# One edge of a fused decoder kernel's first batch: which buffer tile 1's V rows are gathered into, and the order of DVE and TensorE work around it

## The reference

```python
scores = jnp.einsum('bsr,nr->bsn', Q, K) / math.sqrt(K.shape[1])   # 8192 keys per token
topk_scores, topk_idx = jax.lax.top_k(scores, 8)
weights = jax.nn.softmax(topk_scores, axis=-1)
output = jnp.einsum('bskd,bsk->bsd', V[topk_idx], weights)         # 8 rows of V per token
x = _layernorm(x + output)                                         # sublayer 1
q = x @ Wq; k, v = split(context @ Wkv)                            # sublayer 2, 16 heads of 64
attn = softmax(clip(where(mask, q k^T * 64 ** -0.5, max_neg), -5, 5))
x = _layernorm(x + (attn v) @ Wo + bo)
x = _layernorm(x + expert_ffn(x))                                  # sublayer 3
```

## Time and profile before

| | |
|---|---|
| median of 3 runs | 1360.39 us (1360.38 to 1360.89) |
| the profiled execution's own time | 1361.8 us |
| its span, first to last instruction | 1360.0 us |
| PE / DVE / ACT / POOL busy | 1315.0 / 1102.1 / 729.8 / 724.7 us |
| mean granted PE clock over the span | 0.991 of full speed |
| chain that ended last | PE 88%, DVE 8%, the rest 1% or less each |

### The profile page before, as it was taken

One profiled execution on the slowest core, in us unless ns is written; L12 is line 12 of the kernel. 1 busy time (PEld: TensorE's weight loads), 2 busy tenths in 40 slices (PEclk: granted clock), 3 DMA queues, 4 the chain that ended last, 5 costly groups with the idle time before them and its releaser, 6 DMA issues.

```text
span 1360.0 us, 25400 instructions
## 1 busy us (share of the span) xinstructions
PE 1315.0 (97%) x9927; PEld 997.2 (73%) x9927; DVE 1102.1 (81%) x1628; ACT 729.8 (54%) x1377; POOL 724.7 (53%) x1009
## 2 busy tenths in 40 slices
PE   8878999999999999999999999999999999999897
PEld 4556777777878787878787878786868686867775
DVE  2389888888888888888888888888888998546567
ACT  1364555555555555555555555555555554336565
POOL 0553565656565656465656464746574746332425
PEclk8999999999999999999999999999999999999999
DMA  9561121212121212121212121212121316002412
GB/s 369 196 199 58 47 75 55 74 56 75 55 75 55 75 54 75 55 75 55 75 54 75 55 75 55 75 55 75 52 77 36 80 38 183 10 17 95 158 37 90
DMA packets 57554, 110.38 MB, mean 81 GB/s; under 512 B 9443, under 2 KB 38107, under 8 KB 56283
## 3 DMA queue, kind: packets, MB, share of 16 engines
q1 hardware_dynamic: 40326, 62.13, 14.9%
q0 software_dynamic: 14848, 41.96, 10.4%
q10 hardware_dynamic: 2260, 4.66, 0.9%
HBM read 98.50 MB, written 10.22 MB: 80 GB/s over the span
## 4 chain that ended last, share of the span: by engine, by line
PE 88%; DVE 8%; issue 1%; POOL 1%; DMA 1%; ACT 1%; SPq 0%; POOLq 0%; DVEq 0%; ACTq 0%
PE side_bank L390 51%; PE score_bank L390 33%; DVE cand_val L1304 2%; DVE cand_idx L1307 2%; PE score_bank L826 2%; DVE x_sum L1330 1%; DVE dispatchedT L1475 1%; PE side_bank L826 1%; POOL v_rows L1537 1%; DVE x L1368 1%; PE side_bank L553 1%; DMA xT_by_step<-in_xTs 0%; PE score_bank L611 0%; POOL exp L1565 0%; DMA shared_compress<-xT_by_step 0%
## 5 line engine op out<-in xcount | busy, mean ns | idle before, releaser
L976 ACT COPY score_row<-score_bank 128x512 f32<-128x512 f32 x512 | 299.2, 588 | 109.6 <-PE score_bank L390 58.9
L1304 DVE MAX8 cand_val<-score_row 128x8 f32<-128x2048 f32 x128 | 291.8, 2280 | 70.6 <-ACT score_row L976 70.6
L1537 POOL DMA_INDIRECT v_rows<-in_V,top_idx x256 | 248.4, 970 | 122.7 <-issue 70.9
L1565 POOL TENSOR_SCALAR exp<-exp,exp_bound 128x256 f32<-128x256 f32 x512 | 245.1, 495 | 97.3 <-ACT exp L988 95.5
L1307 DVE FIND_INDEX8 cand_idx<-cand_val,score_row 128x8 uint32<-128x2048 f32 x128 | 292.5, 2285 | 0.0
L390 PE MATMUL score_bank<-keysT_hi,qT_hi 128*128 128x512 f32 x512 | 215.5, 421 | 13.0 <-ACT score_row L976 11.9
L390 PE MATMUL score_bank<-keysT_hi,qT_lo 128*128 128x512 f32 x512 | 204.0, 398 | 0.0
L390 PE MATMUL score_bank<-keysT_lo,qT_hi 128*128 128x512 f32 x512 | 203.9, 398 | 0.0
L988 ACT ACTIVATE exp<-side_bank 128x512 f32<-128x512 f32 x256 | 139.0, 595 | 88.3 <-PE side_bank L390 88.3
L390 PE MATMUL side_bank<-qT_heads,kT 64*128 64x256 f32 x1024 | 145.2, 402 | 1.3 <-ACT exp L988 1.3
L1330 DVE SCALAR_TENSOR_TENSOR x_sum<-v_rows,top_weight,x_sum 128x256 f32<-128x256 f32 x256 | 130.0, 508 | 9.2
(11 more groups left out here) (200 smaller groups left out, 2303.5 us busy)
## 6 DMA issues: line engine op xcount, KB each, us to landing
kT<-den_scratch SPq DMA_DIRECT2D x62, 256.0 KB, 4.0
f_quads<-in_f POOLq DMA_DIRECT2D x32, 256.0 KB, 3.4
comp_then_wqkv_raw<-in_comp SPq DMA_DIRECT2D x6, 1024.0 KB, 19.2
xT_by_step<-in_xTs SPq DMA_DIRECT2D x4, 1024.0 KB, 8.8
xT_in<-in_xT SPq DMA_DIRECT2D x16, 256.0 KB, 3.0
keysT_raw<-in_KmT ACTq DMA_DIRECT2D x8, 512.0 KB, 20.6
x_sum<-in_x SPq DMA_DIRECT2D x32, 128.0 KB, 2.0
ctxT_in<-in_ctxT SPq DMA_DIRECT2D x16, 256.0 KB, 4.7
```

Source lines behind the costliest of these rows:

```text
L976: nc.scalar.copy(srow[n // PER % 2][:, i * CB:(i + 1) * CB], scb[n % 3]).then_inc(sem("score_evac"), 1)
L1304: own(nc.vector.max(cv[:, tile, cs], srow[g % 2][:, :]))
L1537: pool.indirect_dma_start(out=vg[:, k, :], out_offset=None, in_=V_rows, in_offset=bass.IndirectOffsetOnAxis(ap=i8[:, tile, k:k + 1], axis=0))\
L1565: last = nc.gpsimd.tensor_scalar(ex[i % NEX][:, k, :], ex[i % NEX][:, k, :], ub[:, k, c:c + 1], E_LO, ALU.min, ALU.max)
```

## The change

Four edits, all of them in turn -1:

1. `gather(0, 1)` writes into `qT_heads` and signals a semaphore of its own (`vg_ramp_in`). It no longer waits for tile 0's sum. `value_sum(0, 1)` reads `qT_heads` in place of `v_rows`.
2. On DVE, `value_sum(0, 0)` goes from behind row 6 to behind row 7 and `merge(0, 1)`. `value_norm(0, 0)` and `x1_lo(0, 0)` go into `first_sum`, the block that holds tile 1's sum, and this block stands between the MAX8 and the FIND_INDEX8 of row 9 in place of row 10.
3. On POOL, `rstd1(0, 0)` goes from ahead of tile 1's gather to behind it.
4. On PE and ACT, row 11's scores go from behind tile 0's transposes to behind the first two query projections. The fills grow from 12 to 20 and from 4 to 8.

```diff
@@ PE, ramp
                 x1_transpose(0, 0)
-                for e in range(4):
-                    score(0, e)
                 project(("K", 0, 2), 1, 4 * P, cth, ctl)
                 project(("K", 0, 3), 1, 6 * P, cth, ctl)
-                fill(12)
+                fill(20)
                 x1_transpose(0, 1)
-                fill(4)
+                fill(8)
                 need(pe, "x1_lo", TT)
                 for j in range(2):
                     project(("Q", 0, j), 0, 2 * j * P, x1h, x1l)
-                for e in range(4, 8):
+                for e in range(8):
                     score(0, e)
@@ ACT, ramp: the same four blocks move behind queries_out(0, 1)
@@ DVE, value_sum
-                    need(dve, "vg_in", 16 * TOPK * (TT * batch + tile + 1))
+                    if in_ramp(batch, tile):
+                        need(dve, "vg_ramp_in", 16 * TOPK)
+                    else:
+                        need(dve, "vg_in", 16 * TOPK * max(TT * batch + tile, 1))
+                rows = qt if in_ramp(batch, tile) else vg
                 for k in ks:
-                    own(nc.vector.scalar_tensor_tensor(acc[:, tile, :], vg[:, k, :], w8[:, tile, k:k + 1],
+                    own(nc.vector.scalar_tensor_tensor(acc[:, tile, :], rows[:, k, :], w8[:, tile, k:k + 1],
@@ DVE, first_sum and the turn
+                value_norm(0, 0)
                 value_sum(0, 1, range(TOPK))
+                x1_lo(0, 0)
                 value_norm(0, 1)
                 x1_lo(0, 1)
...
-                if mid and c:
+                if mid and c > 0:
                     value_sum(m, 0, range(TOPK))
                 candidates(c, 4)
...
                     merge(m, 1)
-                    value_norm(m, 0)
+                    if c == -1:
+                        value_sum(m, 0, range(TOPK))
+                    else:
+                        value_norm(m, 0)
                 candidates(c, 5)
...
-                candidates(c, 6)
-                if c == -1:
-                    x1_lo(m, 0)
-                candidates(c, 7, first_sum if c == -1 else None)
+                candidates(c, 6, first_sum if c == -1 else None)
+                candidates(c, 7)
@@ POOL, gather and the turn
                 if ks[0] == 0:
-                    need(pool, "sum_done", TT * batch + tile)
+                    if in_ramp(batch, tile):
+                        need(pool, "sc_stored", 16 * 4)
+                    else:
+                        need(pool, "sum_done", TT * batch + tile)
                     need(pool, "idx_done", TT * batch + tile + 1)
...
-                    if mid and h == 9 and c != 0:
+                    if mid and h == 9 and c > 0:
                         rstd1(m, 0)
...
+                if c == -1:
+                    rstd1(m, 0)
```

More of the change, by code:

```diff
@@ L250, in need, with in_ramp @@
                 eng.wait_ge(sem(name), v)
+        def in_ramp(batch, tile):
+            return batch == 0 and tile == 1
         def job_bank(key):
@@ L1049, in ramp @@
                 x1_hi(0, 0)
-                for e in range(4):
-                    score_out(0, e)
                 keys_out(0, 2)
@@ L1533, in gather @@
                 if ks[0] == 0:
-                    need(pool, "sum_done", TT * batch + tile)
+                    if in_ramp(batch, tile):
+                        need(pool, "sc_stored", 16 * 4)
+                    else:
+                        need(pool, "sum_done", TT * batch + tile)
                     need(pool, "idx_done", TT * batch + tile + 1)
+                rows, landed = (qt, "vg_ramp_in") if in_ramp(batch, tile) else (vg, "vg_in")
                 for k in ks:
-                    pool.indirect_dma_start(out=vg[:, k, :], out_offset=None, in_=V_rows,
+                    pool.indirect_dma_start(out=rows[:, k, :], out_offset=None, in_=V_rows,
                                             in_offset=bass.IndirectOffsetOnAxis(ap=i8[:, tile, k:k + 1], axis=0))\
-                        .then_inc(sem("vg_in"), 16)
+                        .then_inc(sem(landed), 16)
             def rstd1(batch, tile):
```

## The result

| | before | after |
|---|---|---|
| median of 5 runs each, same chip | 1360.39 us (1360.32 to 1363.87) | 1368.4 us (1366.41 to 1369.64) |
| ratio, with its 95% interval | | 1.004 (1.0025 to 1.0054) |
| span of the profiled execution | 1360.0 us | 1366.6 us |
| PE busy, matmuls | 1315.0 us, 9927 | 1319.1 us, 9951 |

A forecast was written before the change was run, and what follows sets the result against it. PE was taken to bound the kernel from about 141 to 1160 us. Row 11's search, 2.3 us late, would make PE 2.0 late through POOL's clips: 1360.39 + 2.0 = 1362.4 us, range 1359.8 to 1364.3.

The forecast's parts named there:

- DVE's part: In the ramp: tile 1's gather starts at 116.86, its value_norm at 134.73, x1_done comes 4.92 us earlier.
- rival C: In the ramp: tile 1's rows land late or are waited for over 2.5 us; later than 4.2 us, chance 0.04.
- where it is lost: PE's fills hold tile 1's transposes back 2.2 us; row 11's search is 2.3 late, PE 2.0 late through POOL's clips.
- so I take half clock to 131.23: PE's key projections in the ramp: 10 of 24 matmuls at 0.213 us, 14 at 0.120, ending at 132.9.
- rival A: PE in the ramp: half clock stays one more stretch; 3.5 us late in place of 2.0, 1363.9 us; chance 0.22.
- the hole: PE's wait for x1(0, 0) in the ramp, 0.9 us of the half-clock stretch; given as reason for the clock staying low.
- From then on PE, ACT and POOL run in the old pattern, 2.0 us later: After turn 0's products with v: the 2.0 us lateness is carried on, with nothing added in later turns.
- the first paragraph: Takes turn 0's products with v, at 161.71 and 168.71, as PE's last work waiting for something on DVE's schedule.
- The base: The whole kernel's time before the change, 1360.39 us, to which the forecast added 2.0 us.

The follow-up runs named there:

- e3: The changed kernel with 8 and 4 fills in place of 20 and 8; ratio to the kernel before 1.0009, median 1363.44 us.
- e4: The changed kernel, in turn 0 POOL clips heads 2 and 3 ahead of the sixth gather transfer, context's low half behind head 7; ratio 1.0030, 1366.73 us.
- e6_t14: The changed kernel with turn 14's gather split 5, 1 and 2 as in the other turns; ratio to the kernel before 1.0029, median 1366.15 us.
- e2: The changed kernel, unchanged, run once more; ratio to the kernel before 1.0040, median 1367.46 us.
- e7: The changed kernel with 8 and 4 fills, turn 0's changed order of clips and context's low half, and turn 14's gather split; ratio .9992, 1361.11 us.
- e13: The changed kernel with tile 1's transfers counted on the values' own semaphore again, new buffer kept; ratio 1.0024, 1371.74 us on another chip.
- e14: e7 with the values' own semaphore again for tile 1's transfers, new buffer kept; ratio to the kernel before .9976, 1365.78 us on another chip.
- e8: e7 with three of row 11's four blocks ahead of the key projections, 0 and 4 fills; ratio to the kernel before .9993, 1361.57 us.
- e11: The same program as e7, run again; ratio to the kernel before .9980, median 1360.26 us.
- e5: The kernel before with tile 1's gather into the query heads' buffer on its own semaphore, all orders as before; ratio 1.0010, 1363.44 us.
- e9: The kernel before with tile 1's transfers on a semaphore of their own, old buffer kept; one run, 1365.18 us.

## Why the prediction was wrong

**Right: DVE's part.** Less the 1.47 of the start, tile 1's gather began at 116.84 (116.86 forecast) and its layer norm at 134.74 (134.73). The gather was no slower in the other buffer (the layer norm behind it was on time); rival C is out.

**Right: where it is lost.** PE's fills held tile 1's transposes back, DVE idled in front of `x1_lo` (3.96 us), row 11's search was late, and the delay reached PE through POOL's clips. e3 and e4 show both links. PE's waits at turn 0's first products, 0.55 and 1.80 us, are those of the forecast (0.6 and 2.0).

**The step that failed first: "so I take half clock to 131.23".** The low clock lasted to 134.6, rival A's case, which I gave 0.22; 131.23 and the 1.47 of the start make 132.7, so PE had some 1.9 us more at half speed than I allowed. Less the 1.47: fills from 133.83 (forecast 132.9, rival A 134.16), transposes 138.30 (137.35; 138.8), row 11's search 146.79 (145.9; 147.4), batch 1's gather 154.33 (153.45; 155.0), PE in turn 0 2.96 late by the ramp's stage (2.0; 3.5). Everything from there to PE is shifted by the same 0.9 to 1.0.

That the shift stayed under A's 1.5 is luck. In after the low clock began 21.6 us behind row 6: it fell in part on row 10's last block, ahead of a wait, where it costs nothing, and the last five of the 24 key projection matmuls ran at full clock. In e6_t14, the same ramp, it began 23.0 behind and held for all 24. PE's rows there, from tile 0's transposes on:

```profile
128.93 0.69 PE L557 MATMUL side_bank<-identity,x 128*128 128x128 f32 x2 [1.01 <-DVE x L1345]
...
134.54 4.71 PE L394 MATMUL side_bank<-identity 128*128 128x128 f32 x40
139.08 0.38 PE L557 MATMUL side_bank<-identity,x 128*128 128x128 f32 x2
```

Row 6 started at 104.91 there, 0.18 later than before. Less that: fills from 134.36, transposes 138.90, batch 1's gather 154.94 (from 155.12), and the ramp's stage is 3.60 longer than before. A had 134.16, 138.8, 155.0 and 3.5.

Why the clock stayed low is open. A's reason was the hole, PE's wait for tile 0's `x`. In after, e2, e3, e4, e6, e7, e13 and e14 the low clock lasted 6.8 us, in e8 and e11 3.4, and the idle time of PE in the first half does not sort them. These are the first 3.41 us of the low clock in e7, where it stayed, and in e11, the same program, where it went (columns as in the earlier trace rows):

```profile
125.91:129.32 3.41, 3.00 (x10) 2.19 (x11) 3.23 (x6) 1.97 (x5) 0.72 (x2) 0.50 0.23 68
```

```profile
128.00:131.41 3.41, 2.79 (x13) 2.79 (x14) 3.16 (x9) 0.61 (x2) 0.00 (x0) 0.50 0.37 113
```

PE was busy for 3.00 us where the clock stayed low, and for 2.79 where it came back. The Trainium skill (TensorE: Matmul & The Clock Gate, Part 1), that being throttled is the default, had pointed towards A; eight of the ten traces of this ramp agree, and none shows what decides. (The prediction calls on two stretches of the earlier trace rows for it, but only the first of them shows what went ahead of a low clock; for the other the trace has PE busy 1.48 of the 3.42 us ahead.)

**The term that was missing: 1.7 us in turn 14.** "From then on PE, ACT and POOL run in the old pattern, 2.0 us later" is the sentence that failed. It rests on the first paragraph, which took turn 0's products as the last PE work that waits for something on DVE's schedule; the trace before has 2.2 us of such waits in turn 14. I took a second semaphore for a matter of bookkeeping. The late starts were in the trace before (3.82 where 2.40 is usual) and I read past them, because in turn 13 one costs nothing. e5 and e9 show the term alone, 1.3 to 1.4 us. e13 puts the late start back into turn 13; that the time falls with it is likely (2.2 us by the ratios, whose intervals overlap).

**The base.** 1360.39 was the median of three runs that lay within 0.5 us; more runs had a median of 1362.4 to 1363.9 on three chips. By its stages the changed kernel is 4.6 us above whatever that is (2.96 and 1.67), or 5.3 where the low clock falls as in e6 (3.60 and 1.67); by the ratio 5.4, with an interval from 3.4 to 7.3. With the right base, the forecast difference would still have been 2.0 against these 5.4.

## What to carry to other kernels

Work that has been put in to bridge a wait (fills, an early projection) is a fixed cost once the wait is moved: when a change brings data forward, shorten the bridge in the same edit, or the gain ends in front of it. Before adding a semaphore or a transfer to a software queue, look in the old trace for rare long starts on that queue, count their distance, and see which turn they will fall in afterwards. Before pricing an edit from two traces, look where the low clock fell in each. Prove a cause at equal order: a cure that works on the slow kernel has to be tried on the fast one too, since it may cure something else.

## What the hardware showed that was not expected

- Every 56th indirect transfer started 1.42 us late where it headed a gather, and 0.58 late where it stood behind a clip (idle 0.75 where 0.17 is usual); with half the scratch the distance was 28, and two of eight cost nothing (numbers 57 and 169, idle 0.17). The count began anew at transfer 17 when transfers 9 to 16 had used another semaphore, and at transfer 1 otherwise. That a change of semaphore restarts it is the simplest reading of 57 and 73; it was tried with this one pattern only. A separate count of 56 for each semaphore is ruled out: the 57th transfer on the values' own semaphore would have been number 65.
- The same preamble's length differs by up to some 5 us between executions: row 6 was searched from 102.14 in e4 and from 107.69 in e3. An early transfer landed at different times, and PE ran at 1.2 GHz for different stretches (after: 13.7 us from 8.3 on; before: 3.4 at 8.4 and 3.4 at 15.2); how much each of the two costs is not separated. Nothing later gives it back.
- The same program had its clock at 1.2 GHz for 6.8 us at one place in one execution (e7) and for 3.4 in another (e11), and where such a stretch falls moved by up to 1.8 us against the work (21.6 us behind row 6 in after, 23.4 in e11).
- A fill of 128 columns took 0.112 us in a row of 40 ((139.77 - 135.30) / 40), nearly as much as a 256-column matmul of the projections (0.120) at full clock.
